# Keys and values of the second layer computed in the first layer's loop and kept in DRAM, activations handed on through DRAM, four staging slots instead of three

## The reference

```python
# layer 0: x queries, h = [ctx; x] is attended (256 keys), 16 heads of 32
q  = x @ q_w + q_b
kv = concat([ctx, x]) @ kv_w + kv_b
a  = softmax(mask(q k^T / 32)) v @ out_w + out_b + x
n  = rmsnorm(a) * postnorm_w
y  = gelu(n @ w1 + b1) @ w2 + b2 + x
# layer 1: y queries, ctx is attended (128 keys), 32 query heads of 16, 8 key heads
q  = y @ Wq + bq;  k = ctx @ Wk + bk;  v = ctx @ Wv + bv
out = layernorm(softmax(q k^T * scale + mask) v @ Wo + bo + y) * gamma + beta
```

## Time and profile before

| | |
|---|---|
| Three timed runs | 1232.65, 1237.66 (median), 1238.17 us |
| The profiled execution | 1227.86 us, its span 1226.0 us |
| Layer 0, MLP, layer 1 | about 0 to 482, 482 to 856, 856 to 1226 us |
| Busy over the span | PE 89%, DVE 59%, ACT 54%, POOL 33% |
| DMA | 45.91 MB, 37 GB/s in the mean |

### The profile page before, as it was taken

How to read it: one execution, slowest core, us unless ns; L and a number is a source line. 1 busy time by engine, 2 the same in 40 slices (tenths; PEclk the granted TensorE clock), 3 DMA queues, 4 the chain that set the end, 5 groups by cost and what they waited for, 6 DMA issues and landing times. The chain is left out here.

```text
span 1226.0 us, 27214 instructions
## 1 busy us (share of the span) xinstructions
PE 1090.6 (89%) x8976; PEld 919.7 (75%) x8976; DVE 723.3 (59%) x2811; ACT 663.1 (54%) x2204; POOL 404.1 (33%) x539
## 2 busy tenths in 40 slices
PE   4999999999999985899999999998588888888873
PEld 4788888888888874798998998997466666666652
DVE  4577677677777665621221222221589888888882
ACT  4455555555455543733333333332588888888871
POOL 1233333333333341000000000000147676767674
PEclk8999999999999997899999999999699999999986
DMA  8001000000001001600000000020401111111100
GB/s 289 21 1 40 22 19 19 19 19 19 19 19 38 0 2 49 201 18 1 18 17 0 17 17 0 17 70 9 120 23 47 39 45 39 47 36 50 35 18 18
DMA packets 35395, 45.91 MB, mean 37 GB/s; under 512 B 5776, under 2 KB 19344, under 8 KB 35344
## 3 DMA queue, kind: packets, MB, share of 16 engines
q1 hardware_dynamic: 35344, 45.24, 11.4%
HBM read 36.84 MB, written 4.19 MB: 33 GB/s over the span
## 5 line engine op out<-in xcount | busy, mean ns | idle before, releaser
L603 POOL TENSOR_TENSOR pr<-pr,rec 128x512 f32<-128x512 f32 x256 | 260.8, 1039 | 395.3 <-DVE rec L860 395.3
L704 ACT ACTIVATE pr<-pr,nmax 128x128 f32<-128x128 f32 (+1 forms) x768 | 324.5, 428 | 15.5 <-DVE nmax L849 15.4
L849 DVE CUSTOM_DVE_ANT_0 pr<-S,madd 128x128 f32<-128x128 f32 (+1 forms) x768 | 205.2, 330 | 13.2 <-PE S L1039 8.8
L1213 ACT ACTIVATE g_m<-J,b_part_m 128x256 f32<-128x256 f32 x128 | 60.6, 473 | 221.6 <-PE J L161 221.6
L1057 PE MATMUL S<-ident,pr 128*128 128x128 f32 x1024 | 130.5, 276 | 21.1 <-DVE nmax L849 18.0
L704 ACT ACTIVATION_READ_ACCUMULATOR pr<-pr,nmax 128x1 f32 x768 | 147.5, 192 | 0.0
L1057 PEld LDWEIGHTS S<-ident,pr 128*128 128x128 f32 x1024 | 115.7, 142 | 33.5 <-POOL pr L603 26.1
L1191 POOL TENSOR_TENSOR resid_m<-resid_m,b_all_m 128x512 f32<-128x512 f32 x16 | 21.6, 1365 | 325.8 <-DMA resid_m<-in_x 325.7
L866 DVE COPY pT<-S 128x512 f32<-128x512 f32 x128 | 84.0, 685 | 6.3 <-PE S L1057 4.3
L658 ACT ACTIVATE hThi<-J 128x512 fp32r<-128x512 f32 x64 | 38.2, 598 | 86.6 <-PE J L975 86.6
L712 ACT ACTIVATE pT<-S 128x512 f32<-128x512 f32 x128 | 71.6, 585 | 24.2 <-PE S L1057 24.2
(11 more groups left out here) (178 smaller groups left out, 2854.0 us busy)
## 6 DMA issues: line engine op xcount, KB each, us to landing
rows<-in_ctx SPq DMA_DIRECT2D x32, 256.0 KB, 2.6
staged<-in_L_xattn_mlp_w SPq DMA_DIRECT2D x16, 512.0 KB, 3.8
rows<-in_x SPq DMA_DIRECT2D x16, 256.0 KB, 2.9
resid_m<-in_x SPq DMA_DIRECT2D x16, 256.0 KB, 2.7
rows<-between SPq DMA_DIRECT2D x32, 128.0 KB, 2.4
out<-fin SPq DMA_DIRECT2D x16, 256.0 KB, 2.1
between<-in_L_xattn_kv_w SPq DMA_DIRECT2D x4, 512.0 KB, 10.7
mrow<-in_mask_BxS_ik SPq DMA_DIRECT2D x16, 64.0 KB, 3.1
```

The costliest lines, as they stand in the source:

```text
L603: pool.tensor_tensor(part, part, by.unsqueeze(2).broadcast_to([P, per_bank, keys]), ALU.mult).then_inc(normed, 1)
L704: last = nc.scalar.activation(part, part, ACT.Exp, bias=nmax[slot][:, at], scale=-1.0, accum_out=den[slot][:, at])
L849: last = nc.vector.tensor_tensor_reduce(pr[slot][:, j, cols], S[j][:, cols], madd[s][:, :], -1.0, FAR, ALU.add, ALU.min, nmax[slot][:, j * ...
L1213: nc.scalar.activation(g[slot][:, :], J[j][:, 0:PR], ACT.Gelu_apprx_tanh, bias=b1_part[:, f, :]).then_inc(J_taken[j], 1)
```

## The change

The keys and values of layer 1 are computed in the loop of layer 0, where the transposed `ctx` is there already. Two new steps do it, `context` (the product with `[Wk Wv]`) and `turn_context` (the transpose of K and its split), and `keep` stores K and V to DRAM. Layer 1 loads them for each entry and has no `key`, no `turn_key` and no `turn` of `ctx`. `between` is gone: layer 0 stores its output to `kept_n`, the MLP loads it to `n_in` (one buffer of a pair of entries) and stores to `kept_y`, and layer 1 loads that to `y_rows`. SP walks the same list of steps in layer 0. The ring has four slots. The first six units of layer 0 are staged in `pr` and `pT`, and the unit of `[Wk Wv]` and `out_w` in the ring.

```diff
-    SLOTS, SIZE = 3, 1024
+    SLOTS, SIZE = 4, 1024
...
         def first_round(do, b, s, ahead, turned, behind, unfinished):
+            if turned:
+                do["load"](b, s)
...
-            if ahead:
-                do["key"](b + 1, o, 1 - L)
+            if L == 0 and ahead:
+                do["key"](b + 1, o, 1)
             do["mask"](b, s, 1, 1)
             if L == 0 and ahead:
                 do["key"](b + 1, o, 2)
                 do["key"](b + 1, o, 3)
+                do["context"](b + 1, o)
...
                 if ahead:
                     do["value"](b + 1, o, 0)
+                    do["turn_context"](b + 1, o)
+                    do["keep"](b + 1, o)
...
                     do["finish"](b - 1, o)
+                    do["store"](b - 1, o)
             else:
-                if ahead:
-                    do["turn_key"](b + 1, o)
                 if behind:
                     do["output"](b - 1, o)
                 do["exp"](b, s, 1, 1)
                 if turned:
-                    do["turn"](b + 2, s, 0)
+                    do["turn"](b + 2, s, 1)
                 do["probs"](b, s, 0)
-                if turned:
-                    do["turn"](b + 2, s, 1)
                 do["exp"](b, s, 1, 2)
                 do["normalise"](b, s, 1, 0)
                 if turned:
-                    do["turn_low"](b + 2, s, 0)
                     do["turn_low"](b + 2, s, 1)
...
+                def keep(b, s):
+                    sp.wait_ge(*turned_context[0])
+                    for h in range(2):
+                        sp.dma_start(kept_k[b, h], CT[s][h][:, :, :].bitcast(F32)).then_inc(sems["kv_stored"][s], 16)
+                    sp.dma_start(kept_v[b], CV[s][:, :, :, :]).then_inc(sems["kv_stored"][s], 16)
...
+                    def load_values_next(b, s):
+                        taken = b * ROUNDS + ROUNDS
+                        sp.wait_ge(O_taken, taken if isinstance(b, int) else sp.snap(taken))
+                        load_values(b + 2, s)
...
+                    with sp.Fori(0, (B - 4) // 2) as it:
+                        for s in range(2):
+                            load_values_next(it * 2 + s + 1, 1 - s)
+                            load(it * 2 + s + 2, s)
+                            store_out(it * 2 + s, s)
...
+                def context(b, s):
+                    j, n = w.use("J", 2)
+                    natural["context"] = (J_taken[j], n + 1)
+                    pe.wait_ge(J_taken[j], n)
+                    split_product(nc, J[j][:, 0:2 * KW1], lambda h, k: hT[h][:, k, 0, :],
+                                  lambda h, k: wc[h][:, k, :], KC).then_inc(J_full[j], 1)
...
                 def prepare(i, t):
-                    nc.scalar.activation(nT[t][0][:, :, :], between[:, :, bass.ds(i * PR, PR)], ACT.Copy)\
+                    act.wait_ge(sems["n_loaded"], i * 32 + 32)
+                    nc.scalar.activation(nT[t][0][:, :, :], n_in[:, :, :], ACT.Copy)\
                         .then_inc(n_hi, 1)
```

More of the change, by code:

```diff
@@ L190, in xattn_kernel, with engine_ops, attention @@
                       (H, [(every, None, by_chunk(w2)[:, half[u]])], 1)]
-        KW1 = KV1 * DH1
         o_rows = Wo.rearrange("(g c d) n -> g d c n", c=GROUPS1, d=DH1)
         part2 = [(H, [(every, None, by_chunk(Wq)[:, half[u]])], 1) for u in range(2)]
-        part2 += [(2 * KW1, [(every, slice(0, KW1), by_chunk(Wk)), (every, slice(KW1, 2 * KW1), by_chunk(Wv))], 1)]
         part2 += [(H, [(slice(DH1 * g, DH1 * (g + 1)), None, o_rows[g][:, half[u]]) for g in range(KV1)], 1)
                   for u in range(2)]
[L198 to L206, removed]
+        staging = Staging(nc, top, [part0, part1, part2], 6)
+        attention(nc, top, staging, 0, ident, handed, banks, x, ctx_rows, key_mask, q_b0,
+                  (kv_b0, bk, bv), out_b0, post_w0, None, None)
+        mlp(nc, top, staging, handed, S, J, x, b1, b2)
+        attention(nc, top, staging, 1, ident, handed, banks, x, ctx_rows, add_mask, bq,
+                  None, bo, gamma, beta, out)
+OPS = ("weights", "weights_ready", "turn", "turn_low", "query", "key", "value", "turn_query", "context",
+       "turn_context", "scores", "mask", "exp", "normalise", "probs", "values", "output", "moments", "root",
+       "norm", "affine", "residual", "projected", "finish", "load", "keep", "store")
+def engine_ops(**own):
+    assert set(own) <= set(OPS)
+    return dict.fromkeys(OPS, lambda *_: None) | own
+def attention(nc, top, staging, L, ident, handed, banks, x, ctx_rows, mask, q_b, kv_b, o_b,
               norm_w, norm_b, out):
     S, J, O, T = banks
+    (kept_n, kept_y, kept_k, kept_v), n_in, y_rows, sems = handed
     st = ExitStack()
@@ L561, in _ @@
+                    load_weights(WEIGHTS["context"])
+                    load_weights(WEIGHTS["out"])
                     for u in staging.prefetched(1):
                         staging.load(sp, u)
-                load_next(0, 0)
-                load_next(1, 1)
-                with sp.Fori(0, (B - 4) // 2) as it:
+                    all_entries(sp, w, engine_ops(turn=uses_j, query=uses_j, key=uses_j, value=uses_j, context=uses_j,
+                                                  turn_context=turn_context, output=uses_j, turn_query=uses_t,
+                                                  finish=finish, load=load, keep=keep, store=store))
@@ L636, in affine @@
                             .then_inc(fin_ready, 1)
[L638 to L645 removed]
+                all_entries(pool, w, engine_ops(normalise=normalise, residual=residual, root=root, affine=affine))
             @block.scalar
@@ L1097, in finish, with mlp @@
                         mm.then_inc(T_full, 1)
[L1099 to L1109 removed]
+                all_entries(pe, w, engine_ops(weights_ready=weights_ready, turn=turn, query=query, key=key, value=value,
+                                              turn_query=turn_query, context=context, turn_context=turn_context,
+                                              scores=scores, probs=probs, values=values, output=output,
+                                              finish=finish, projected=projected))
+def mlp(nc, top, staging, handed, S, J, x, b1, b2):
+    (kept_n, kept_y, _, _), n_in, y_rows, sems = handed
     PAIRS, PR = B // 2, 2 * R
@@ L1129, in mlp @@
         resid = [sb(f"resid{t}", [P, H]) for t in range(2)]
+        y_out = [sb(f"y_out{r}", [P, H]) for r in range(2)]
         consts_loaded = sem("consts_loaded")
```

416 lines of the change are left out of this document (244 added, 172 removed).

## The result

The changed kernel took 1282.41, 1291.05 (median) and 1291.94 us, against 1232.65 to 1238.17 of the kernel before: 1.0448 times as long, 95% interval 1.0401 to 1.0494. I had said 1271 with a range of 1254 to 1284. The sign was right. The size was not, and the result is outside the range. The profiled execution is one of 1291.05 us, so against the profiled 1227.86 of before the kernel grew by 63.2 us, where my sum was 35.2.

A forecast was written before the change was run, and what follows sets the result against it. PE was taken to bound layer 0 and the MLP, and a round between engines layer 1. Layer 0 +52.2, MLP +1.8, layer 1's start 0 and entries -18.8 gave +35.2 us: 1271 us forecast, range 1254 to 1284.

The forecast's parts named there:

- I take 1.25 us for an entry: Layer 1: each of entries 1 to 13 gets 1.25 us shorter, a new wait at `turn` included.
- the -18.8 of the sum: Layer 1 in all: 13 x 1.25 + 1.8 for entry 0 + 0.7 for entry 14, 18.8 us less.
- the two pieces: Layer 1's entry: `output` starts 0.72 us earlier, and DVE loses one `hTlo` and a wait for ACT; 1.56 together.
- the wait for `y_rows`: Layer 1: PE waits 0.3 us at `turn` for rows loaded behind V, bounds 0 and 0.9.
- layer 1 giving less: Rival: POOL's run or slow row loads limit layer 1; an entry gains only 0.5 us, sum +45, 1281 us; chance 0.15.
- +52.2: Layer 0 in all: fourteen entries with 1.5 for `context` and 1.85 bank wait, entry 0 1.7, prologue 3.6.
- the wait for V: Layer 0: the second `value` product shares a bank, so PE waits 1.85 us for DVE to read the first.
- the other terms of the prologue: Layer 0's prologue, besides 1.1 for one more weight unit: the product 1.5, the second `turn` in the same bank 1.0.
- +1.8: MLP: the later `n_in` load, partly offset by the fourth staging slot, adds 1.8 us, bounds 0 and 3.3.
- the fourth slot: MLP start: a fourth staging slot has the fourth weight unit ready, giving back some of the 3.3 us added.
- the rival that rested on its one buffer: Rival: the MLP waits 2.6 us for `n_in` in each of seven pairs, +18, 1289 us; chance 0.03.
- Two rivals, at 1231 and 1247: 1231: layer 1 falls to its engines' work, -7, chance 0.03. 1247: no bank wait in layer 0, +9, chance 0.04.

The follow-up runs named there:

- all three edits: Changed kernel with twelve filler matmuls ahead of `output`, rows loaded ahead of V, and `moments` with one SBUF tensor input, all in layer 1: 1265.78 us, 1.0266.
- the filler alone: Changed kernel with twelve extra matmuls that feed nothing, on PE ahead of `output` in layer 1: 1280.6 us, 1.0376.

## Why the prediction was wrong

**The step that failed is "I take 1.25 us for an entry"** of layer 1, the -18.8 of the sum, which came out at +6.8. Its two gains are real in the main: with all three edits a cycle takes 1.20 us less than before, of the 1.56 that the two pieces were to give. Three things took them back.

1. The clock. The sum had no term for it. The work that left the round stood ahead of `output`, and where PE idles 1.9 us instead, the granted clock falls to its lower level for up to 3.5 us in seven cycles of twelve. With the filler alone layer 1 shortens by 346.2 - 335.3 = 10.9 us. That the missing work of PE is the cause is shown by putting work there (all cycles at 1.00) and by taking it away again (eleven of twelve at 0.92). That it is the length of the idle stretch, and not that PE is busy for less of the whole cycle, is argued from the place where the clock falls: the filler changes both (190.5 us busy of 246.6, and 201.6 of 240.1), and no run separates them. At the start of the block the clock is lower too, 0.88 from the first `normalise` to the first `fin`, where it was 1.00. Why a given cycle falls and the next doesn't stays open: in the changed kernel long and short cycles follow each other in no order that I can see, with the rows loaded earlier every third is short.
2. The rows and DVE's held operation. At the full clock they are worth 20.0 - 19.02 = 1.0 us a cycle, and 335.3 - 322.2 = 13.1 us in the block. Of these I had named the wait for `y_rows`, at 0.3 with a bound of 0.9. It costs 0.5 (20.0 to 19.5 in the run with the load moved). The held operation was in no term: `hTlo` left DVE's queue, so `moments` came earlier, into POOL's normalise. Before, DVE came to that operation at 1016.68, when POOL's normalise (1014.67 + 2.04 = 1016.71) was all but over:

```profile
1016.68 0.16 DVE L915 TENSOR_TENSOR stat<-stat 128x1 f32<-128x1 f32 x1
...
1014.67 2.04 POOL L603 TENSOR_TENSOR pr<-pr,rec 128x512 f32<-128x512 f32 x2 [1.22 <-DVE rec L860]
```

Before, the operation ended 0.13 us behind POOL's, and now it ends 0.01 us behind it, though DVE comes to it 0.9 us sooner in POOL's run. So what DVE won by having one `hTlo` less was lost there.

3. Both work on each other. Each edit that shortened the round without the filler led to more cycles at the lower clock and so to little or no gain in time (1284.97 and 1287.01 us alone, 1281.91 together). A single experiment read by its median alone would have acquitted both.

10.9 and 13.1 are 24.0 of the 25.6 us. The split depends on the order: taken the other way round it is 5.3 for the rows and the small operations (346.2 - 340.9) and 18.8 for the clock.

Of the rivals, layer 1 giving less (0.15) was the direction, but by another mechanism. In the twelve cycles of the changed kernel PE never waits for POOL's normalise. With the three edits it does, 0.34 us in each, so POOL's run comes onto the round once the other causes are gone. That is less than half of the 0.75 us an entry that the rival charged to it. I had given layer 1 a worst case of some 9 us less, and nothing in my list let it get slower. That is why the range was too short at its upper end.

**Layer 0, right in its mechanism, and lucky in its size: +55.7 for +52.2.** An entry grew by 3.01 us (I said 3.35), with the wait for V at 1.58 (1.85), the product at 1.49 (1.5). The transpose fitted into the wait. Fourteen such entries are 4.8 us less than I had, and what lies before and behind them grew by 13.6 us (55.7 - 14 x 3.01) where I had 5.3. The two misses nearly cancel. The first scores, for which I had allowed 1.1 (the other terms of the prologue stand behind them), came 4.97 us later, at 36.76 instead of 31.79. Of that, 2.4 is the new wait of POOL for `bc_all`, which put its residual beside DVE's splits. The clock took a share here too, for which I had no term: `query` of entry 1 begins at 50.47 with a matmul every 0.43 us, at a granted clock of 0.51, and takes 4.5 us instead of 3.0. The last entries cost some 2.5 us more than I had, which I haven't taken apart.

**The MLP, right: +0.6 for +1.8.** Its first step waited 4.50 us for `n_in` and began 5.10 us behind the end of layer 0 instead of 1.17, 3.9 us later where I had 3.3. The first gelu came 14.38 us behind that end instead of 13.39, +1.0. So 2.9 us came back by then, where I had 1.5 for the fourth slot, and a little more came back later. No later step waited for `n_in`, so the rival that rested on its one buffer fell.

**The start of layer 1**, which I took at 0, was -0.5: the first `normalise` comes 30.84 us behind the end of the MLP's last write (942.91 - 910.68 - 1.39) instead of 31.29 (887.04 - 854.36 - 1.39).

**The timed runs.** The profiled executions differ by 63.2 us, the medians by 53.4. That of before was a fast one, 9.8 us below its median, and that of the changed kernel is its median, so all of the 9.8 went, of which I had taken off 2. Later series put the kernel before at 1231.6 to 1234.3, so its three runs were a little high. The sum was 28 us short and the forecast missed the median by only 20: that part is luck. Two rivals, at 1231 and 1247, were added to the median of before without the 2 us that I had taken off the others. On the same footing they are 1229 and 1245.

## What to carry to other kernels

Work taken out of a round leaves a hole on its engine. If the engine is PE, ask whether the clock still holds over the hole. If it doesn't, the product behind it takes half as long again, and that may be more than was won. When an engine comes earlier to its next piece, look at what the other engines do at that new time. Small DVE operations with two SBUF tensor inputs are cheap only where POOL is quiet, and a scalar operand for each partition does the same without the hold. And when several causes take a gain in turn, remove them together once: alone, each seems innocent.

## What the runs showed of the hardware

- DVE's operations of 128x1 with two SBUF tensor inputs took 0.62 to 0.97 us under a normalise of POOL and 0.15 to 0.22 without. Written with one tensor input and a scalar operand from SBUF they took 0.20 to 0.27 under it. 128x512 splits took 1.75 us beside POOL's residual and 0.69 without. The Trainium skill (SBUF — State Buffer, SBUF: two separate sides) says that DVE and POOL share a pair of ports as an exclusive lock, which a DVE operation with two SBUF inputs needs for its whole length. The runs agree: the operation of 0.94 us ended at 1056.21, and POOL's normalise at 1056.20.
- 1.9 us of idle PE between products was enough for `output` to begin at 1.2 GHz in 7 of 12 cycles, and in all 12 in the run with the small operations rewritten. With 1.69 us of matmuls in the hole it did in none of the 12. The Trainium skill (TensorE: Matmul & The Clock Gate, Part 1) says that the throttled state is the default and that activity releases it. The rows agree: in those cycles the granted clock behind the idle stretch was 0.50, and with matmuls in the stretch it was 1.00.
- Twelve extra matmuls in each cycle made the kernel faster: 6.5 us in twelve cycles, and 18.8 us over the block where the other two causes were gone.
